# Two-layer graph attention kernel: the odd slot's VectorE list reordered, every norm product on GpSimd, other lists for the first and last graphs

## What is computed

```python
h = jnp.maximum(_layernorm(x), 0.0)
x = x + _L0_gnn_ref(h, adj, ...)
h = jnp.maximum(_layernorm(x), 0.0)
x = x + _L1_gnn_ref(h, adj, ...)

def _L0_gnn_ref(embs, score_mask, ...):                 # 8 heads of 64
    m = embs @ map_w.T + map_b
    sem = heads(m)
    norm = jnp.maximum(jnp.linalg.norm(sem, axis=-1, keepdims=True), COS_EPS)
    n = sem / norm
    cos = jnp.einsum('bhsd,bhtd->bhst', n, n) * ~sm
    cos_adj = cos > 0.1
    q, k = heads(m @ q_w.T + q_b), heads(m @ k_w.T + k_b)
    p_attn = softmax(where(sm, NEG, q k^T / 8)) * keep
    adj = cos_adj * p_attn
    Ax = adj @ heads(embs @ gcn_map_w.T + gcn_map_b)
    return relu((Ax @ gcn_W.T) / (adj.sum(-1) + 1.0))

def _L1_gnn_ref(x, adjacency_mask, ...):                # 4 heads of 64
    q, k, v = heads(x @ Wq), heads(x @ Wk), heads(x @ Wv)
    attn = softmax(where(adjacency_mask, q k^T / 8, -max))
    return (attn @ v) @ Wo + bo
```

## Time and profile before

| | before |
|---|---|
| median of 3 runs | 2554.92 us (2554.35 to 2557.24) |
| the profiled execution's own time | 2557.17 us |
| its span, first to last instruction | 2555.3 us |
| PE busy | 2460.2 us, 96% |
| PE weight loads | 1967.7 us, 77% |
| DVE busy | 2142.0 us, 84% |
| ACT busy | 1940.6 us, 76% |
| POOL busy | 2130.0 us, 83% |
| mean granted TensorE clock | 0.994 |

### The profile page before, as it was taken

One profiled execution on the slowest core, in us unless ns is written; L12 is line 12 of the kernel. 1 busy time (PEld: TensorE's weight loads), 2 busy tenths in 40 slices (PEclk: granted clock), 3 DMA queues, 4 the chain that ended last, 5 costly groups with the idle time before them and its releaser, 6 DMA issues.

```text
span 2555.3 us, 77639 instructions
## 1 busy us (share of the span) xinstructions
PE 2460.2 (96%) x29624; PEld 1967.7 (77%) x29624; DVE 2142.0 (84%) x3490; ACT 1940.6 (76%) x5032; POOL 2130.0 (83%) x2259
## 2 busy tenths in 40 slices
PE   8899999999999999999999999999999999999996
PEld 6677777777778778778777777777777787787775
DVE  6888888888888888888888888888888888888886
ACT  6687787787777777877877877877877777778765
POOL 3788888888888888888888888888888888888875
PEclk9899999999999999999999999999999999999999
DMA  6567767768767777678777777677777677786753
GB/s 167 120 126 149 154 132 150 144 141 155 140 144 155 140 144 150 142 142 154 131 147 155 132 152 152 135 151 144 141 155 141 144 155 140 144 151 140 145 120 73
DMA packets 855921, 364.02 MB, mean 142 GB/s; under 512 B 781440, under 2 KB 789120, under 8 KB 855552
## 3 DMA queue, kind: packets, MB, share of 16 engines
q1 hardware_dynamic: 855552, 359.06, 70.6%
HBM read 142.91 MB, written 34.08 MB: 69 GB/s over the span
## 4 chain that ended last, share of the span: by engine, by line
PE 76%; POOL 7%; ACT 7%; issue 4%; DVE 3%; DMA 1%; SPq 1%; ACTq 0%; DVEq 0%; POOLq 0%
PE unit_ps L1915 22%; PE unit_ps L1929 21%; PE unit_ps L2087 21%; PE s_ps L1939 3%; PE s_ps L1992 3%; PE c_ps L1939 3%; ACT e_ec L946 3%; POOL e_ec L733 2%; PE unit_ps L2059 1%; ACT least L957 1%; PE unit_ps L1939 1%; POOL p_hl L728 1%; POOL qk_hl L754 1%; DVE o_sb L1418 1%; PE unit_ps L2003 1%
## 5 line engine op out<-in xcount | busy, mean ns | idle before, releaser
L946 ACT ACTIVATE e_ec<-e_ec,neg_mx 128x128 f32<-128x128 f32 x1008 | 390.0, 388 | 4.1
L2087 PE MATMUL unit_ps<-m_hl,w_k_hi 128*128 128x256 f16 x2048 | 359.8, 274 | 6.3 <-DVE qk_sb L1343 6.3
L1052 ACT ACTIVATE qk_hl<-qk_sb 128x512 f16<-128x512 f32 x256 | 153.3, 622 | 275.5 <-DVE qk_sb L1343 275.5
L2087 PE MATMUL unit_ps<-m_hl,w_q_hi 128*128 128x256 f16 x2048 | 356.6, 273 | 0.0
L1915 PE MATMUL unit_ps<-h_t,w_m_hi 128*128 128x256 f16 x2048 | 342.4, 274 | 1.0 <-issue 1.0
L1929 PE MATMUL unit_ps<-w_v_hi,h_t 128*128 128x512 f16 x1024 | 325.1, 379 | 0.0
L1307 DVE SCALAR_TENSOR_TENSOR e_ec<-c_ps,e_ec 128x1024 f32<-128x1024 f32 x126 | 154.3, 1225 | 188.1 <-ACT e_ec L946 188.1
L733 POOL TENSOR_TENSOR e_ec<-e_ec 128x1024 f16<-128x1024 f32 x126 | 296.6, 2354 | 7.2 <-ACT e_ec L986 4.5
L1915 PE MATMUL unit_ps<-h_t,w_m_lo 128*128 128x256 f16 x1024 | 280.5, 274 | 0.0
L1013 ACT ACTIVATE h_sb<-x,shift,rstd 128x512 f32<-128x512 f32 x128 | 104.1, 814 | 196.3 <-POOL shift L811 196.3
L2087 PE MATMUL unit_ps<-m_hl,w_k_lo 128*128 128x256 f16 x1024 | 240.1, 275 | 0.0
(11 more groups left out here) (275 smaller groups left out, 7657.1 us busy)
## 6 DMA issues: line engine op xcount, KB each, us to landing
norm_n<-norm_d SPq DMA_DIRECT2D x128, 512.0 KB, 4.9
xa<-in_x_dram SPq DMA_DIRECT2D x128, 256.0 KB, 3.2
x<-in_x_dram SPq DMA_DIRECT2D x128, 256.0 KB, 2.9
out_dram<-x SPq DMA_DIRECT2D x128, 256.0 KB, 2.7
h_t<-h_hl SPq DMA_TRANSPOSE x254, 3.5
ec_t<-e_ec SPq DMA_TRANSPOSE x252, 3.4
adj_in<-in_adj_dram SPq DMA_DIRECT2D x128, 16.0 KB, 2.1
p_t<-p_hl SPq DMA_TRANSPOSE x126, 3.3
```

Of the source, the lines that this page charges most:

```text
L946: ins = nc.scalar.activation(e[:, h, :], e[:, h, :], ACT.Exp, bias=neg[:, h:h + 1], scale=SCALE, accum_out=sums[:, h:h + 1])
L1052: nc.scalar.activation(dst[:, 0, c, :], src[:, c, :], ACT.Copy).then_inc(done, 1)
L2087: ins = nc.tensor.matmul(ps[:, c % 2 * 2 * P:(c % 2 + 1) * 2 * P], w[a][:, i, c * P:(c + 1) * P], parts[:, b, i, :], start=n == 0, stop=n ...
```

## The change

- `threshold` on ACT is gone, and with it the 8 instructions at the head of every even slot and of slot 0. POOL makes `least` for every graph: for an even graph at the end of the odd slot ahead of it, for graph 0 ahead of slot 0.
- DVE's list in an odd slot has another order: `o1_rows(s, 4)`, `norm_sums` and `attended` stand ahead of `gate`, which comes just before `k_features(0)`. For slot z the same.
- Slots 0 to 3 have other lists: in slots 1 and 3 both `q_features` stand ahead of `above`; `e_upper` and `e_lower` come ahead of the squares and of the threshold in slots 0 and 2; layer 1's weights are split into their parts one or two slots later; `square_rest` moves behind `v_features`, in slot 0 into slot 1.
- In the last slots `e_lower(z)` no longer waits for `k_lo`, and `result(z)` comes ahead of `attended(a)`.

```diff
--- before.py
+++ after.py
@@ -786,7 +786,7 @@
                 g = s.n % 2
                 pool.wait_ge(norm_in[g], s.at(lambda t: 16 * (t // 2 + 1)))
                 pool.wait_ge(norm_done, s.at(lambda t: t // 2 + 1))
-                pool.wait_ge(lowered, s.at(lambda t: t))
+                wait(pool, lowered, s.at(lambda t: t))
                 nc.gpsimd.tensor_tensor(least[:, :, :], norm_n[:, g].rearrange("p n h -> p h n"),
                                         norm[:, g * H:(g + 1) * H].unsqueeze(2).broadcast_to([P, H, P]),
                                         ALU.mult).then_inc(threshold_done, 1)
@@ -840,14 +840,15 @@
                     result_base(s)
                     norm_l1(s)
                     o1_lower(s, 4)
+                    threshold(Slot(s.n + 1, None, B))
                 elif s.n == 0:
                     v_lower(s)
                     keep_row(s)
                     block_mask(s)
                     m_lower(s)
                     norm_l0(s)
+                    e_lower(s)
                     threshold(Slot(s.n + 1, None, B))
-                    e_lower(s)
                 elif s.n == 2:
                     h1_lower(s)
                     m_lower(s)
@@ -886,6 +887,7 @@
             pool.wait_ge(ones_in, ONES)
             norm_rows(before_0)
             q_lower(before_0, 1)
+            threshold(Slot(0, None, B))
             pool.wait_ge(bo_in, 16)
             over_slots(pool, B, slot)
             z, a, b, c, d, e, f, g = late_slots(B)
@@ -896,7 +898,6 @@
             q_lower(z, 0)
             norm_rows(z)
             q_lower(z, 1)
-            pool.wait_ge(k_lo, 2 * (B // 2))
             e_lower(z)
             threshold(a)
             norm_l1(z)
@@ -947,16 +948,6 @@
                                                    accum_out=sums[:, h:h + 1])
                 ins.then_inc(done, 1)
 
-            def threshold(s):
-                if s.has(0):
-                    g = s.n % 2
-                    act.wait_ge(norm_in[g], s.at(lambda t: 16 * (t // 2 + 1)))
-                    act.wait_ge(norm_done, s.at(lambda t: t // 2 + 1))
-                    wait(act, lowered, s.at(lambda t: t))
-                    for h in range(H):
-                        ins = nc.scalar.activation(least[:, h, :], norm_n[:, g, :, h], ACT.Copy, scale=norm[:, g * H + h:g * H + h + 1])
-                    ins.then_inc(threshold_done, 1)
-
             def scores_exp(s):
                 if s.has(0):
                     wait(act, den_done, s.at(lambda t: t - 1))
@@ -1086,37 +1077,36 @@
                     qk_upper(s, "q", q_sb, q_hl, 0, q_hi)
                     qk_upper(s, "q", q_sb, q_hl, 1, q_hi)
                     e_upper(s)
+                    if s.n == 1:
+                        l1_weights_upper(0)
+                        l1_weights_upper(1)
                     o1_upper(s, 4)
                     qk_upper(s, "k", k_sb, k_hl, 0, k_hi)
+                    if s.n == 1:
+                        l1_weights_upper(2)
                     lqk_upper(s, "lq", lq_hl, LQ)
                     qk_upper(s, "k", k_sb, k_hl, 1, k_hi)
                     lqk_upper(s, "lk", lk_hl, LK)
                     h1_rows(s)
                     h1_upper(s)
                 elif s.n == 0:
-                    threshold(s)
                     m_upper(s)
                     scores_exp(s)
+                    e_upper(s)
                     squares(s)
-                    e_upper(s)
-                    l1_weights_upper(0)
-                    l1_weights_upper(1)
                     v_upper(s, "va", 2)
                     v_upper(s, "vb", 3)
-                    l1_weights_upper(2)
-                    l1_weights_upper(3)
                 elif s.n == 2:
                     m_upper(s)
-                    threshold(s)
                     scores_exp(s)
+                    e_upper(s)
                     squares(s)
-                    e_upper(s)
                     v_upper(s, "va", 2)
+                    l1_weights_upper(3)
                     h1_rows(s)
                     h1_upper(s)
                     v_upper(s, "vb", 3)
                 else:
-                    threshold(s)
                     scores_exp(s)
                     l1_exp(s, 4)
                     e_upper(s)
@@ -1509,39 +1499,55 @@
                 v_features(s, "va", 0)
                 x_stats(s)
                 gate(s)
-                square_rest(s)
                 v_features(s, "vb", 1)
-                l1_weights_lower(0)
 
             def slot(s):
                 if s.n == 0:
                     first_slot(s)
+                    return
+                if s.n == 1:
+                    scores_mask(s)
+                    square_rest(Slot(0, None, B))
+                    q_features(s, 0)
+                    q_features(s, 1)
+                    above(s)
+                    norm_sums(s)
+                    attended(s)
+                    gate(s)
+                    k_features(s, 0)
+                    l1_weights_lower(0)
+                    x1_stats(s)
+                    k_lower(s, 0)
+                    k_features(s, 1)
+                    k_lower(s, 1)
                     return
                 if s.n == 2:
                     m_features(s, 0)
                     l1_weights_lower(1)
                     m_features(s, 1)
+                elif s.n == 3:
+                    q_features(s, 0)
                 scores_mask(s)
                 if s.odd:
-                    q_features(s, 0)
-                    o1_rows(s, 5)
-                    above(s)
-                    q_features(s, 1)
-                    if s.n == 1:
-                        norm_sums(s)
-                    elif s.n == 3:
-                        l1_weights_lower(3)
+                    if s.n == 3:
+                        q_features(s, 1)
+                        above(s)
+                    else:
+                        q_features(s, 0)
+                        o1_rows(s, 5)
+                        above(s)
+                        q_features(s, 1)
+                    o1_rows(s, 4)
+                    norm_sums(s)
+                    attended(s)
                     gate(s)
-                    o1_rows(s, 4)
-                    if s.n > 1:
-                        norm_sums(s)
-                        attended(s)
-                        k_features(s, 0)
-                    else:
-                        k_features(s, 0)
-                        attended(s)
+                    if s.n == 3:
+                        l1_weights_lower(2)
+                    k_features(s, 0)
                     x1_stats(s)
                     k_lower(s, 0)
+                    if s.n == 3:
+                        l1_weights_lower(3)
                     lqk_lower(s, "lq", lq_hl, LQ, 0)
                     k_features(s, 1)
                     k_lower(s, 1)
@@ -1551,12 +1557,11 @@
                     attended(s)
                     x1_stats(s)
                     above(s)
-                    l1_weights_lower(2)
                     gate(s)
                     v_features(s, "va", 0)
                     x_stats(s)
+                    v_features(s, "vb", 1)
                     square_rest(s)
-                    v_features(s, "vb", 1)
                 else:
                     l1_mask(s, 4)
                     l1_max(s, 4)
@@ -1783,10 +1788,10 @@
             o1_rows(z, 5)
             above(z)
             q_features(z, 1)
-            gate(z)
             o1_rows(z, 4)
             norm_sums(z)
             attended(z)
+            gate(z)
             k_features(z, 0)
             k_lower(z, 0)
             k_features(z, 1)
@@ -1797,9 +1802,9 @@
             above(a)
             scores_mask(b)
             gate(a)
+            result(z)
             attended(a)
             x1_stats(a)
-            result(z)
             above(b)
             gate(b)
             lqk_lower(z, "lk", lk_hl, LK, 1)
```

## The result

| | before, same chip | changed |
|---|---|---|
| median of 6 runs | 2555.28 us (2554.35 to 2557.24) | 2565.48 us (2564.88 to 2567.22) |
| ratio | | 1.004, 95% interval 1.0027 to 1.0053 |
| forecast | | 2576 us (2549 to 2609), slower |
| DVE, ACT, POOL busy | 2142, 1941, 2130 us | 2122, 1729, 2261 us |

The kernel became slower, by 10.2 us where 21 were forecast. The sign and the mechanism held; the size was twice what was measured. Medians are over all runs; only the kernel with the new lists alone, in the table of experiments, had runs far from the others, two of eleven (4217 and 14416 us), without which its median is 0.1 us lower. The page of the changed kernel: busy times, and the chain of work that ended last.

A forecast was written before the change was run, and what follows sets the result against it. ACT's even-list loop was taken to bind at 38.72 us; POOL's list then takes over at 39.17. 60 pairs times 0.45 give +27, start -5, end -1: +21 us, so a median of 2576 us, range 2549 to 2609.

The forecast's parts named there:

- POOL takes over: Steady pairs: POOL's list, with one more 2.47 us product, becomes the binding loop; pair goes from 38.72 to 39.17 us.
- its wait for o_hl: Sign in POOL's trace: its wait of 1.86 us for ACT's o_hl stays in the changed kernel.
- Two signs: Trace signs: POOL busy about 2285 us; PE waits about 1.3 us a pair ahead of q01 for POOL's m_lower.
- The loop's length: POOL's loop per pair: 8.16 + 30.53 - 1.85 + 2.47 - 0.17 = 39.14 us, 39.17 with 0.03 to wake ACT.
- Port waits: POOL's losses to DVE instructions reading two SBUF tensors: 1.44 us a pair instead of 1.61.
- The rival that norm_rows holds the port as well: First k_lower beside norm_rows costs POOL 0.44 us more: pair 39.6, 2602 us; chance 0.17, shared with late norms.
- Late norms: POOL's product waiting for its norms: none counted, upper end 1.1 us a pair, at most 2642 us; chance 0.17, shared.
- Start: First slots: PE's waits of 2.65 and 3.10 us in slots 1 and 3 go; between 0 and -10, taken -5 us.
- End: Last slots: PE and DVE run further ahead of POOL, wait for k_lo leaves e_lower(z); -1 us, between -3 and +1.
- What bounded the kernel before: Closed loop over ACT's even list, through lv_upper, square_rest and POOL's L811, without slack, holds the pair at 38.72 us.
- PE's need: PE per pair: 38.72 less its 0.83 us wait ahead of lq, 37.89 us.
- the third rival: PE binds: without port waits POOL's loop is 37.73 us, so PE sets the pair at 37.9; 2499 us; chance 0.15.

The follow-up runs named there:

- the kernel with the new lists alone: Kernel before with only the new lists of the first and last slots; from slot 4 products on ACT and gate as before: 2552.9 us, ratio 0.9985.
- a second product: Changed kernel with the even graphs' product (slots 4 to 124) done once more on POOL into an unread tile: 2728.1 us, ratio 1.0674.
- the reorder alone: Changed kernel with the even graphs' products from slot 4 on back on ACT, so new lists and gate order only: 2536.4 us, ratio 0.9922.

## Why the prediction was half right

- **That POOL takes over, and the product is why: right.** POOL has no wait in its stretch, its wait for o_hl stays at 1.87 us, ACT waits 5.47 us (6 forecast), and a second product shows in full. Two signs failed: POOL is busy for 2261 us instead of about 2285, and ahead of q01 PE waits for m_lower for 22.8 us in all, 0.4 a pair, where 1.3 a pair were forecast.
- **The loop's length: the term that was mis-sized.** Of the sum, 30.53 - 1.85 + 2.47 - 0.17, with the 0.03, gives 31.01 us from o1_lower(5) to ACT's h1_rows; the rows show 1233.73 - 1202.94 = 30.79. The prediction added durations and took off the idle times of the brackets. On this engine a large instruction that follows without a wait starts about 0.05 us before the one ahead ends by the trace, so a filled wait gives back more than its bracket. Taken from start to start: o1_lower(4) to h1_lower 1.64 before, 3.04 now, +1.40 where 1.51 was counted; result_base to the odd product 1.46 to 1.23, -0.23 where 0.18 was; the odd product to p1_lower 3.18 to 2.42, -0.76 where 0.71 was. That is 0.21 of the 0.22 us. The pair grew by 0.22 us where 0.45 were forecast, so the loop costs 59 x 0.22 = 13 us and not 27. In a difference of two loops of 39 us, an error of 0.5% in one is as large as what is left.
- **Port waits: right** (0.45 for e_lower, nothing beside norm_rows, 0.99 for p1_lower: 1.44 us, as forecast). The rival that norm_rows holds the port as well is out: 0.69 us beside it.
- **Late norms: between.** I counted none; seven pairs of 59 lose 2.6 us. The other end, 1.1 us in each pair, was never near.
- **Start: right in size** (-3.9 for -5, of which the preparation ahead of slot 0, 0.5 us, isn't the lists' doing). **End: -3.6 for -1.** 2.4 us of it come from the slots before; PE enters the tail ahead of POOL, but that this is their cause is argued. By the traces the miss is 21 - 8.2: 14 us too much for the loop and 2.6 too little saved at the end, less 2.6 for the late norms and 1.1 at the start. That the three smaller ones nearly cancel is luck.
- **What bounded the kernel before: partly wrong.** The loop went through POOL's odd half too. It didn't change the forecast of this kernel, in which that loop is open anyway (ACT waits 4.25 and 5.47 us for POOL), but by it the reorder alone was mispredicted (2548 for 2536).
- **PE's need: 37.68, not 37.89 us.** It had no part in the sum, only in the third rival.

## What to carry to other kernels

Where two loops lie within a per cent of each other, measure a moved instruction from start to start in the trace and walk the whole loop over every engine it passes, not the list of one: here that would have given +13 instead of +27 us for the steady part. An instruction put into a wait costs less than its length, and the same instruction a few rows further down costs all of it plus the wait. When an operation binds whichever engine has it whole, divide it: three heads of eight on GpSimd and five on ScalarE gave 2490 us, where the whole on either gave 2536 and 2565.
